# A third PSUM bank in ScalarE's ring, and layer 0's products taken from two SBUF tiles, in a CIN recommendation tower

## The reference, cut to what matters

```python
e = jnp.stack([tbl_0[ids[:, 0]], ..., tbl_31[ids[:, 31]]], axis=1)      # 512 x 32 x 32

def _cin_forward(inputs, filters):                                     # filters: (1, 1024, 128), (1, 4096, 128)
    x0 = inputs
    prev = inputs
    outs = []
    for W in filters:
        z = jnp.einsum('bhd,bmd->bhmd', x0, prev)
        b, h, m, d = z.shape
        z = z.reshape(b, h * m, d)
        cur = jnp.einsum('bpd,pn->bnd', z, W[0])
        cur = jax.nn.relu(cur)
        prev = cur
        outs.append(cur)
    result = jnp.concatenate(outs, axis=1)
    return jnp.sum(result, axis=-1)

h = jnp.concatenate([z, dense_ctx], axis=1)
h = jnp.maximum(h @ W_top1 + b_top1, 0.0)
h = jnp.maximum(h @ W_top2 + b_top2, 0.0)
y = h @ W_top3                                                          # 512 x 1
```

## Time and profile before

| | us |
|---|---|
| median of 3 runs | 954.28 (953.75 to 955.1) |
| the profiled execution, its own time | 953.77 |
| its span, first to last instruction | 951.8 |
| chunks' matmuls, start to end (83 to 928 us of the span) | about 845 |

### The profile page before, as it was taken

One profiled execution on the slowest core, in us unless ns is written; L12 is line 12 of the kernel. 1 busy time (PEld: TensorE's weight loads), 2 busy tenths in 40 slices (PEclk: granted clock), 3 DMA queues, 4 the chain that ended last, 5 costly groups with the idle time before them and its releaser, 6 DMA issues.

```text
span 951.8 us, 14370 instructions
## 1 busy us (share of the span) xinstructions
PE 867.6 (91%) x3572; PEld 660.0 (69%) x3572; DVE 760.1 (80%) x2380; ACT 763.3 (80%) x2559; POOL 680.0 (71%) x650
## 2 busy tenths in 40 slices
PE   0326999999999999999999999989999999999997
PEld 0114777777777777767777777767777777777763
DVE  0123798896889999887888999978898899998882
ACT  1316998987888989888888898888888889989852
POOL 6772888786878888885788788865666666676560
PEclk9999999999999999999999999999999999999999
DMA  9045666666666666666666666666566666665430
GB/s 263 12 125 154 153 149 152 144 151 162 149 156 158 149 144 140 155 143 149 158 147 162 160 147 148 140 153 143 145 158 152 147 159 149 140 143 109 84 73 0
DMA packets 57718, 133.84 MB, mean 141 GB/s; under 512 B 8785, under 2 KB 22321, under 8 KB 57538
## 3 DMA queue, kind: packets, MB, share of 16 engines
q0 software_dynamic: 22528, 69.22, 38.8%
q1 hardware_dynamic: 32178, 59.94, 19.6%
q10 hardware_dynamic: 2928, 3.76, 1.3%
HBM read 62.64 MB, written 5.24 MB: 71 GB/s over the span
## 4 chain that ended last, share of the span: by engine, by line
PE 82%; issue 9%; POOL 3%; ACT 2%; DVE 2%; another core or an unknown queue 1%; DMA 1%; POOLq 0%; DVEq 0%; ACTq 0%
PE ya L651 15%; PE ya L652 13%; PE ya L653 13%; PE yd L651 10%; PE yd L652 10%; PE yd L653 10%; PE acc L652 3%; PE acc L651 3%; PE acc L653 3%; ACT scaled L439 1%; POOL quarter L305 1%; PE acc L674 1%; PE ya L750 1%; DVE acc L568 1%
## 5 line engine op out<-in xcount | busy, mean ns | idle before, releaser
L439 ACT ACTIVATE scaled<-ya,emb 128x128 f32<-128x128 f32 x2304 | 645.9, 386 | 91.8 <-PE ya L653 84.1
L568 DVE SCALAR_TENSOR_TENSOR acc<-yd,emb,acc 128x128 f32<-128x128 f32 x1408 | 394.7, 343 | 51.6 <-PE yd L653 51.4
L651 PE MATMUL ya<-w_hi,prev_hi 128*128 128x512 f32 x576 | 243.2, 422 | 11.0 <-DVE prev_lo L534 5.4
L305 POOL TENSOR_TENSOR quarter<-scaled 128x512 f32<-128x512 f32 x128 | 197.9, 1546 | 71.0 <-DMA scaled<-scaled 51.4
L652 PE MATMUL ya<-w_lo,prev_hi 128*128 128x512 f32 x576 | 227.4, 395 | 0.0
L653 PE MATMUL ya<-w_hi,prev_lo 128*128 128x512 f32 x576 | 226.8, 394 | 0.0
L298 POOL DMA_DIRECT2D scaled<-scaled x128 | 117.6, 919 | 119.3 <-ACT scaled L439 112.6
L651 PE MATMUL yd<-w_hi,prev_hi 128*128 128x512 f32 x448 | 176.7, 394 | 1.8 <-DVE pooled_b L587 1.5
L652 PE MATMUL yd<-w_lo,prev_hi 128*128 128x512 f32 x448 | 175.7, 392 | 0.0
L653 PE MATMUL yd<-w_hi,prev_lo 128*128 128x512 f32 x448 | 175.7, 392 | 0.0
L651 PEld LDWEIGHTS ya<-w_hi,prev_hi 128*128 128x128 f32 x576 | 108.6, 189 | 83.0 <-ACT scaled L439 37.8
(11 more groups left out here) (68 smaller groups left out, 719.9 us busy)
## 6 DMA issues: line engine op xcount, KB each, us to landing
scaled<-scaled POOLq DMA_DIRECT2D x128, 512.0 KB, 8.1
xb<-xt_scratch SPq DMA_DIRECT2D x64, 512.0 KB
x<-xt_scratch SPq DMA_DIRECT2D x64, 192.0 KB
xm<-xt_scratch SPq DMA_DIRECT2D x32, 256.0 KB
emb<-in_tbl,idx POOLq DMA_INDIRECT x128, 4.0
scaled<-in_L_rec_filter SPq DMA_DIRECT2D x8, 256.0 KB
xt_scratch<-xt_stage SPq DMA_DIRECT2D x7, 256.0 KB
xt_scratch<-xt_stage SPq DMA_DIRECT2D x9, 128.0 KB
```

The source lines that it names most:

```text
L305: pool.tensor_tensor(four, piece[:, 0:C], piece[:, C:2 * C], ALU.add).then_inc(quartered, 1)
L439: op = act.activation(scaled[:, tile % PR, C * j + N * i:C * j + N * (i + 1)], ya[:, n % RA, N * i:N * (i + 1)], ACT.Copy, scale=scale_of( ...
L568: dve.scalar_tensor_tensor(after, y_part, scale_of(tile, HB * j + i), before, ALU.mult, ALU.add).then_inc(chained, 1)
L651: pe.matmul(dst, v_hi, m_hi, start=start, stop=False)
```

## The change

It does four things: the ring `ya` gets a third bank (`RA` 2 to 3); the PSUM bank `xm_ps` and ACT's `copy_xm` are gone; DVE's product reads both factors from SBUF; and `xm` has two buffers, the load of chunk c into one of them waiting for the products of chunk c-2.

```diff
-    RD, RA = 3, 2
+    RD, RA = 3, 3
...
-        xm_ps = psum("xm_ps", [P, C])
...
-        xm = sb("xm", [P, C])
+        xm = sb("xm", [P, 2, C])
...
-        xm_loaded = sem("xm_loaded")
+        xm_loaded = [sem(f"xm_loaded_{r}") for r in range(2)]
...
-        xm_in_psum = sem("xm_in_psum")
...
             def load_xm(c):
-                if c > 0:
-                    sp.wait_ge(xm_in_psum, c)
-                sp.dma_start(xm[:], dram(xt, c * CH, [[C, F], [0, 4], [1, C]])).then_inc(xm_loaded, 16)
+                if c > 1:
+                    sp.wait_ge(product_ready, KT * (c - 1))
+                sp.dma_start(xm[:, c % 2, :], dram(xt, c * CH, [[C, F], [0, 4], [1, C]])).then_inc(xm_loaded[c % 2], 16)
...
-            def copy_xm(c):
-                act.wait_ge(xm_loaded, 16 * (c + 1))
-                if c > 0:
-                    act.wait_ge(product_ready, KT * c)
-                act.activation(xm_ps[:], xm[:], ACT.Copy).then_inc(xm_in_psum, 1)
...
-            copy_xm(0)
...
-            copy_xm(1)
...
-                            if (q, j) == (2, 0):
-                                copy_xm(c + 2)
...
             def product(c, k):
                 n = KT * c + k
                 if k == 0:
-                    dve.wait_ge(xm_in_psum, c + 1)
+                    dve.wait_ge(xm_loaded[c % 2], 16 * (c // 2 + 1))
...
-                dve.tensor_tensor(prod[:], xb[:, k, :], xm_ps[:], ALU.mult).then_inc(product_ready, 1)
+                dve.tensor_tensor(prod[:], xb[:, k, :], xm[:, c % 2, :], ALU.mult).then_inc(product_ready, 1)
```

## The result

The changed kernel takes 965.34 us (median of 4 runs, 961.55 to 966.03); beside it on the same chip the kernel before took 954.69 us. The ratio is 1.0105, with a 95% interval from 1.0081 to 1.0129: slower by 1.0%. The forecast was 939 us, its range 920 to 962, and it gave 0.21 to "slower". The kernel before took 950.7 to 954.8 us on the chips of the later experiments, so those are compared by their ratio to it.

What follows compares the result with a forecast made beforehand. PE was taken as the bound, with 4.0% of a regular stretch stalled for lack of a buffer. The span, 951.8 - 32 + 1 + 16 = 936.8 us, plus 2.0 around it, gave about 939 us, range 920 to 962.

Steps and rivals of the forecast that it cites:

- "slower": Whole kernel slower by more than 0.2% (1.9 us): the every-POOL-instruction rival and part of the runs-of-adds rival, chance 0.21.
- The third bank: PE's weight loads for `ya` no longer wait for ACT's scaling: minus 32 us, bounds 0 and 32.
- The rival that ACT would be short of time: ACT late by throughput among its small steps, half the stalls stay: 939 us with no collision, chance 0.05.
- The copy: 32 x 646 ns leave ACT, already hidden in its waits for PE: 0 by itself.
- The turns: PE's 2.18 us wait for ACT's sort before each of three turns may grow: plus 1 us, bounds 0 and 3.
- The rule of one add: A DVE product starting inside a POOL tensor add waits for that add's end: 30.4 us of waits, 939 us, chance 0.40.
- the runs of adds: Rival: DVE's product waits until a whole unbroken run of POOL adds ends: 52.5 us of waits, about 950 us, chance 0.20.
- the 30.4 us: Summed waits of DVE's products for one POOL add each; a chunk's four get 0.22, 0.63, 0.04 and 0.09 us.
- the forecast's line: PE's new wait for the third `lo`: 0.72 + 0.89 - 1.09 = 0.52 us a chunk, times 31: plus 16 us.
- POOL's DMA instructions taking part: Rival: every POOL instruction, DMA included, shuts DVE's product out: 956 to 992 us, middle 974, chance 0.15.
- The break-even that it named: Third `lo` 1.4 us late a chunk makes PE wait 1.03 us, the whole gain, and decides against the change.

Runs made afterwards that it cites:

- experiment 1: Changed kernel, but every product after the first takes its second factor from PSUM bank `prod` (values wrong): 920.83 us, ratio 0.9639.
- experiment 3: Changed kernel with the product's second factor from PSUM (values wrong) and two A banks, so the kernel before without ACT's copy: 954.72 us, ratio 1.0002.
- experiment 6: Changed kernel with layer 0's first and third triple moved later on PE, to (0, 3) and (1, 4): 950.93 us, ratio 0.9971.
- experiment 10: Changed kernel with layer 0's first, third and fourth triple moved later on PE, to (0, 3), (1, 4) and (2, 3): 944.33 us, ratio 0.9921.
- experiment 7: Changed kernel with one of the 14 D banks of a chunk given to ACT instead of DVE: 958.94 us, ratio 1.0065.
- Experiment 2: Changed kernel with the A ring back at two banks, the product still from SBUF alone: 984.23 us, ratio 1.0309.
- experiment 5: Changed kernel with second factor from PSUM (values wrong), plus idle DVE subtractions ahead of products 0, 1 and 2 of each chunk: 952.5 us, ratio 0.9989.

## Why the prediction was wrong

**The third bank: right, and in size.** Minus 32 us were forecast; experiment 1 against experiment 3 shows 34 us, and a matmul distance of 0.2262 us, which is the 0.2265 of the earlier trace rows. The rival that ACT would be short of time fell with it.

**The copy: right.** Experiment 3: nothing.

**The turns: right in being small.** PE's three waits for the sort sum to 6.8 us (22.8 us in four, less the 16.0 us of the first), against 3 x 2.18.

**The rule of one add: right for most of the loss.** In the changed kernel 69 products end 0.55 to 0.57 us after the end of the POOL add that they started inside, also where POOL's next add follows at once. They lost 44.4 of the 53.7 us. Each loses the rest of that one add less 0.13 us. So it is the likeliest case of the forecast and not the runs of adds. POOL's indirect gathers (L280) take no part: 11 products start inside one and no add, and lose at most 0.01 us each. The 27 products that overlap no add took 690 to 701 ns, against 694 on average before, so two SBUF operands have no price of their own here. The other 9.0 us were lost by 13 products that ended later than that, most of it by six; they stand in the last section. The sum of all times from a product's start to the end of its add, 55.7 us over 89 products, is near 53.7 partly by luck: the 0.13 us that each does not lose and the 9.0 us nearly cancel. (Products and adds whose starts agree to 0.01 us are left out of the 89.)

The Trainium skill's rule in SBUF — State Buffer, "Who interferes with whom", that the later of the two waits for the earlier, agrees: the product started at 457.39 waits for the add of 457.07, and the add of 458.83 waits for the product. By the recorded starts it does not hold for all products, as the last section shows, and there the measurement decides.

**The step that failed: the 30.4 us.** It was found by laying the products over POOL's adds as both stood in the trace of before. By place in the chunk I took 0.22, 0.63, 0.04 and 0.09 us; measured were 0.21, 0.64, 0.77 and 0.06. Three of four are right to 0.03 us, which is partly luck as well, since in the changed kernel more products meet an add and each loses less than its rest. The third product had started just as an add ended, 0.04 us on average; but the first two are themselves late by 0.85 us. The trace of before says what that does: with the third product of each chunk moved 0.7 to 0.9 us later over the same adds, the add that it starts inside has 1.1 to 1.3 us left on average. With each delay handed on to the later products of the chunk, the same trace gives 0.21, 0.45, 0.50 and 0.21 us, 43.8 us in all. That is still short, as POOL's adds move too and some products wait longer, but it shows the failure: a collision moves what comes after it, and the phases of before can't be kept for the instructions behind the first one.

**How it reached PE: right in part, and a second way was put at nothing.** With the measured losses the forecast's line reads 0.72 + 0.21 + 0.64 + 0.77 - 1.09 = 1.25 us a chunk, 39 us in place of 16, and the time 923 + 39 = 962 us, against 965 measured. With that one term mended the sum comes out on the right side, but that it comes so near is luck, as the line puts all 39 us down to `lo`. The table takes every distance between two starts on PE within the chunks, less 0.2262 us, and sums it by what the later matmul writes (us, turns left out):

| | A banks | D banks | layer 0 |
|---|---|---|---|
| before | 38.8 | 9.6 | 1.0 |
| experiment 1, no collision | 5.1 | 6.0 | 5.1 |
| changed kernel | 7.0 | 20.7 | 30.2 |
| experiment 6, two triples later | 7.4 | 22.6 | 21.0 |
| experiment 10, three triples later | 8.3 | 20.3 | 18.7 |
| experiment 7, a D bank less | 14.1 | 8.6 | 32.6 |

The third bank takes the A banks' 38.8 us away. The collision then adds 25 us at layer 0, where `lo` is late, and 15 us at D banks, which DVE gives back late because the products stand before them in its queue. The forecast had no term for the D banks. Experiments 6 and 10 give PE more time before it needs `lo` and win back 13 and 18 us of the 44.5 (1.3% and 1.8%); in their traces it is layer 0's part that falls. Experiment 7 takes the D banks' part away and leaves layer 0's.

**The rivals.** "Slower" was put mostly on POOL's DMA instructions taking part, at 0.15; they did not have to. The break-even that it named, 1.4 us of delay by the third `lo`, was the right test: measured are 0.21 + 0.64 + 0.77 = 1.62. Slower was not a far case but the likeliest mechanism with a shifted phase: with a third product that collides as the second one does, 0.63 in place of 0.04, the same working gives 957 us. That is still inside the range; the measured 965 is not, as the third product lost 0.77 us and the D banks were put at nothing.

## What to carry to other kernels

When two engines collide on a resource, count the collisions of the first instruction of a chunk from the old trace, but hand each delay on to the later ones, and try their starts at several shifts: here that turned 0.04 us into 0.5 to 1.3. Ask of every instruction behind the delayed one who waits for it, not only of the next in its own chain. Before giving up a PSUM operand of VectorE that keeps it clear of GpSimd, add up how long GpSimd's adds run; here 0.42 us a product turned a gain of 3.6% into a loss of 1.0%. And a stall from two uses of a ring in a row may be had away by order: other work put between them brought 2.7%, with no bank added.

## What the runs showed of the hardware that was not expected

The longest product of the changed kernel, on DVE, and POOL beside it:

```profile
189.74 2.81 DVE L513 TENSOR_TENSOR prod<-xb,xm 128x512 f32<-128x512 f32 x1
```

```profile
188.44 1.35 POOL L328 TENSOR_TENSOR small_split<-small,small_split 32x512 fp32r<-32x512 f32 x1
189.69 0.98 POOL L296 DMA_DIRECT2D scaled<-scaled  x1
190.32 1.67 POOL L303 TENSOR_TENSOR quarter<-scaled 128x512 f32<-128x512 f32 x1
```

The product starts 0.05 us before an add ends, and could have gone on at 189.79. It ends at 192.55, 0.56 us after the end of the next add at 191.99, although that one is recorded only from 190.32. Another product starts inside no add at all, and waits too:

```profile
270.94 2.23 DVE L513 TENSOR_TENSOR prod<-xb,xm 128x512 f32<-128x512 f32 x1
```

```profile
270.36 0.91 POOL L296 DMA_DIRECT2D scaled<-scaled  x1 [0.94 <-ACT scaled L431]
271.00 1.60 POOL L303 TENSOR_TENSOR quarter<-scaled 128x512 f32<-128x512 f32 x1
```

It starts inside the DMA issue of L296, 0.06 us ahead of the add, and ends 0.57 us after that add. Experiment 2 has ten such products, 0.10 to 0.18 us ahead of the add, which lost 1.6 us each, and three that start at the beginning of the same issue, 0.56 to 0.60 us ahead of the add, and lost nothing. Yet in the changed kernel the product of 133.77, inside the same issue and recorded within 0.01 us of the start of its add, went first, and the add took 1.85 us. So the order of the recorded starts does not say which of the two goes first, and the DMA issue as a whole does not keep the product out. Whether the add claims its turn before its recorded start or the later part of the issue does, these records can't tell apart. Twelve of the 127 products took over 1.0 us more than 694 ns, eight of them by the rule of one add alone.

It was also not expected that time put on DVE costs so much while DVE still waits for PE elsewhere: 0.7 us for each microsecond in experiment 5, with DVE waiting 42.5 us for PE in that same run. The average idle share of an engine says little about a delay that stands in the one stretch of the chunk where it has no wait.
